# Graph attention with a residual layer norm on one core: x loads and result stores of two 128-row tiles instead of one

## The chip, the cores and the metric

The kernel runs on one core of a Trainium2 chip. The metric is the device time of one execution in microseconds (us), the median over several runs. Before the change it is 457.74 us, the median of three runs that lie between 457.65 and 457.76.

## What is computed

N = 4096 rows, D = 512 columns, all in float32. Cut to what matters:

```python
q = x @ Wq.T + bq
k = key @ Wk.T + bk
v = value @ Wv.T + bv
scores = (q @ k.T) / N ** 0.5
s = scores * adj                                   # adj is 0 or 1 and sparse
s = where(abs(s) < 1e-5, -1e9, s)
y = softmax(s, axis=-1) @ v @ Wm.T + bm
out = layernorm(x + y)
```

## The kernel before, in words

The rows of x are dealt to T = 35 tiles of R = 118 rows, padded to 128 rows in DRAM, so that each tile meets at most 256 distinct columns of the adjacency. The program has two halves.

**First half.** TensorE (PE) multiplies Wv by Wm (line 635) and then the values by the product (line 584, `value_rows`), giving a table of 4096 x 512 that ScalarE (ACT) stores to DRAM. Meanwhile GpSimd (POOL) loads the adjacency tiles (`load_adj`, line 461, 944 KB each after the cast), and VectorE (DVE) reduces each to a list of the columns in use (`reduce_tile`, line 1077 and after).

**Second half.** A loop `for i in range(T + 1)`, written out once per engine, works on one tile per step. Step i holds, on PE: the transposes of the gathered key rows and adjacency columns of tile i + 1 (lines 694, 704), the product with the values of tile i - 2 (line 737), four matmuls of a query block (`project`, line 594), the scores of tile i + 1 (line 713), and the transposes of the probabilities of tile i (line 724). POOL gathers keys six tiles ahead, values up to three. DVE does `soften(i)`, in which `key_bias(i + 1)` (line 1199) is the first reader of the x tile i + 1, and `add_x(i - 2)` (line 1288), which adds the x tile to the attention output, writes `y_buf`, and is the last reader of that x tile. From step 31 on, `add_x` is one tile nearer. ACT normalises finished tiles (`finish`, line 969), four per group of statistics.

**The queue around the change.** SyncE (SP) only issues DMAs, in the order of its own program, and blocks on each wait. It starts with the weights, then `load_x` for the first XB tiles. Then in step i it issues `store(t)` for the tiles that `finish_of(i - 1)` names, in every fourth step `load_xT` (the transposed x of four tiles for the query block, line 408), and `load_x(i + XB - 1)`. The waits are these:

```python
def load_x(t):
    if t >= XB:
        sp.wait_ge(y_sb, t - XB + 1)          # add_x of the tile that held the buffer
def store(t):
    sp.wait_ge(fin_sb, t + 1)                 # ACT has normalised tile t
# DVE, key_bias(t):   dve.wait_ge(x_in[t % XB], 16 * (t // XB + 1))
# DVE, add_x(t):      dve.wait_ge(stored[t % YB], 16 * (t // YB))   for t >= YB
```

`x_buf` has XB = 5 tiles of 2 KB per partition, `y_buf` YB = 8. The last tile is stored in two halves of its columns, one by ACT (line 965) and one by SP (line 436); after that SP waits for all stores (line 440). The code under `overflow` handles a graph that does not fit the lists; with these inputs it does not run.

Of the kernel before, what the change touches and what calls it, by code (L numbers as in the profile page):

```python
# [12 lines left out]
P = 128  # L13
N = 4096
D = 512
DC = D // P
T = 35
TP = 36
R = 118
ROWS = T * P  # L20
QR = 4 * R
# [22 lines left out]
AD = 6  # L44
XB = 5
YB = 8
# [25 lines left out]
def build(nc, adj_tiles, adj_cols, key, valueT, x, xT, wq, wk, wv, wmT, bm, consts, table, out):  # L72
    with ExitStack() as ctx:
# [3 lines left out]
        def sem(name):  # L77
            return ctx.enter_context(nc.semaphore(name))
# [106 lines left out]
        cols_in = [sem(f"cols_in{i}") for i in range(2)]  # L185
        x_in = [sem(f"x_in{i}") for i in range(XB)]
        adj_gathered = [sem(f"adj_gathered{i}") for i in range(AD)]
        key_gathered = [sem(f"key_gathered{i}") for i in range(KD)]
        v_gathered = [sem(f"v_gathered{i}") for i in range(VD)]
        stored = [sem(f"stored{i}") for i in range(YB)]  # L190

# [106 lines left out]

        x_tiles = x.rearrange("(t r) d -> t r d", r=P)
        out_tiles = out.rearrange("(t r) d -> t r d", r=P)  # L300
        table_blocks = table.rearrange("(b r k) d -> b r k d", k=4, r=P)
# [17 lines left out]

        def one_tile(ap, t):  # L320
            return ap[bass.ds(t, 1)].rearrange("a p d -> p (a d)")

        def wait_apart(eng, s, value):
            eng.wait_ge(s, value)
            eng.sem_inc(passed, 1)
# [78 lines left out]
        @block.sync  # L404
        def _(sp):
            def load_xT(nb):
                sp.wait_ge(q_ps, DC * (nb - 1))
                sp.dma_start(xT_buf[nb % 2], xT[nb]).then_inc(cols_in[nb % 2], 16)

            def load_x(t):  # L410
                if t >= XB:
                    sp.wait_ge(y_sb, t - XB + 1)
                sp.dma_start(x_buf[:, t % XB, :], x_tiles[t]).then_inc(x_in[t % XB], 16)

            def store(t):
                sp.wait_ge(fin_sb, t + 1)
                sp.dma_start(out_tiles[t], y_buf[:, t % YB, :]).then_inc(stored[t % YB], 16)

            for e in range(DC):
                sp.dma_start(v_left[:, e, :], wv[e * P:(e + 1) * P, :]).then_inc(weights2_in[e], 16)  # L420
            sp.dma_start(cst[:, :], consts).then_inc(cst_in, 16)
            sp.dma_start(bm_row[:, :], bm).then_inc(bm_in, 16)
            sp.dma_start(w_left, wq.rearrange("(e p) d -> p e d", p=P)).then_inc(weights_in, 16)
            sp.dma_start(w_right, wk.rearrange("(e p) d -> p e d", p=P)).then_inc(weights_in, 16)
            for t in range(XB):
                load_x(t)
            for i in range(T + 1):
                for t in finish_of(i - 1):
                    store(t)
                if i % 4 == 0 and i // 4 + 2 < QBL:  # L430
                    load_xT(i // 4 + 2)
                if i >= 1 and i + XB - 1 < T:
                    load_x(i + XB - 1)
            store(T - 2)
            sp.wait_ge(last_sb, 1)
            sp.dma_start(out_tiles[T - 1][:, HD:D], y_buf[:, (T - 1) % YB, HD:D]).then_inc(stored[(T - 1) % YB], 16)
            sp.wait_ge(rounds_ready, 1)
            rounds = sp.value_load(rounds_i[0:1, 0:1], min_val=0, max_val=MAXR)
            for i in range(YB):
                sp.wait_ge(stored[i], 16 * (len(range(i, T, YB)) + (i == (T - 1) % YB)))  # L440
            sp.sem_inc(again, 1)

            with overflow(sp, rounds) as n:
                with sp.Fori(0, n) as r:
                    with sp.Fori(0, QBL) as nb:
                        wait_apart(sp, g_q_sb, (r * QBL + nb) * DC + 1)
                        sp.dma_start(g_xT, xT[bass.ds(nb, 1)].rearrange("a p d n -> p (a d) n")).then_inc(g_xT_in, 16)
                sp.wait_ge(g_p_all, 2)
                with sp.Fori(0, T) as t:
                    sp.dma_start(y_buf[:, 0, :], one_tile(x_tiles, t)).then_inc(g_x_in, 16)  # L450
                    wait_apart(sp, g_fin, t + 1)
                    sp.dma_start(one_tile(out_tiles, t), y_buf[:, 1, :]).then_inc(g_stored, 16)
                    wait_apart(sp, g_stored, t * 16 + 16)

# [389 lines left out]
        def _(act):  # L844
# [114 lines left out]
            def finish_half(t):  # L959
# [4 lines left out]
                act.wait_ge(fin_sb, T)  # L964
                act.dma_start(out_tiles[t][:, 0:HD], y_buf[:, t % YB, 0:HD]).then_inc(stored[t % YB], 16)

# [70 lines left out]
        def _(dve):  # L1037
# [156 lines left out]
            def key_bias(t):  # L1194

                dve.wait_ge(x_in[t % XB], 16 * (t // XB + 1))
                if t >= 1:
# [81 lines left out]
            def add_x(t):  # L1279
# [4 lines left out]
                if t >= YB:  # L1284
                    dve.wait_ge(stored[t % YB], 16 * (t // YB))
                dve.wait_ge(r_denom_sb, t + 1)
# [199 lines left out]
def layout(rows, adj, key, value, x, Wq, Wk, Wv, Wm, bq, bk, bv, bm):  # L1486
# [25 lines left out]
    for i, b in enumerate((bq, bk, bv)):  # L1512
# [5 lines left out]
        "valueT": np.ascontiguousarray(value.reshape(NB, P, 4, DC, P).transpose(0, 4, 3, 2, 1)).reshape(NB, P, DC, 512),  # L1518
        "x": x_rows[:T].reshape(ROWS, D),
        "xT": np.ascontiguousarray(x_rows[:, :R].reshape(QBL, QR, DC, P).transpose(0, 3, 2, 1)),  # L1520
# [28 lines left out]
```

## Time and profile before

| | |
|---|---|
| median of three runs | 457.74 us |
| span of the profiled execution | 486.1 us |
| PE busy | 444.0 us, 91% of the span |
| DVE / ACT / POOL busy | 65% / 39% / 51% |
| DMA queue of SP (q1) | 12866 packets, 28.51 MB, 16.4% of the 16 engines' span |
| DMA queue of POOL (q0) | 18480 packets, 70.45 MB, 57.6% |
| x loads, result stores | 35 and 34 DMAs of 256 KB, one packet of 2 KB per partition |

The profiled execution is another execution than the timed ones and carries the recording. Its own time is given only as its span, from the first to the last instruction; that span is 28.4 us longer than the median. In the views a row has the line of the kernel, the engine, the operation, what is written and read, and its busy time. A DMA queue's share is the time of its packets over the time of 16 DMA engines. What the page calls "another core or an unknown queue" (`remote` in a wait) is a wait whose releasing event the records do not tell.

### The profile page before, as it was taken

Reading aid. Unit: us, or ns where it says so; the run is one execution under the profiler, and the core shown is the slowest. Engines: PE = TensorE matmul, PEld = TensorE weight load, DVE = VectorE, ACT = ScalarE, POOL = GpSimd, SP = SyncE. Lnnn points to the kernel's source line nnn. Section 1 sums busy time; section 2 is a strip of 40 time slices with the busy share of each in tenths; the row PEclk is TensorE's granted clock in tenths of the full one; section 3 lists DMA queues with packets and bytes.
Section 4 is the critical chain, followed back from the end, with each engine's and each line's share of the span. In section 5 each row is a group of like instructions: output and inputs, shape, how many; then the busy total and the mean of one; then the engine's idle time right before and its main releaser. Section 6 shows DMA issues by size and latency. Waiting matters only on the chain.

```text
span 486.1 us, 5650 instructions
## 1 busy us (share of the span) xinstructions
PE 444.0 (91%) x1536; PEld 246.8 (51%) x1536; DVE 317.3 (65%) x923; ACT 191.2 (39%) x447; POOL 248.6 (51%) x251
## 2 busy tenths in 40 slices
PE   9999999999999889999889798998979899889982
PEld 5444444444444455666455465655645455555651
DVE  0258535993487067989997685976937675435684
ACT  1232413433341433434443353453444345335573
POOL 2110005007672166877777776766766666661410
PEclk9999999999999998999999899999989999998997
DMA  8999999999999999998999866999757566562553
GB/s 329 363 221 285 283 290 257 226 267 316 332 311 343 268 281 241 248 285 242 229 239 321 267 188 241 257 249 324 200 150 245 166 204 227 165 212 80 156 188 112
DMA packets 34693, 119.25 MB, mean 245 GB/s; under 512 B 6767, under 2 KB 7023, under 8 KB 32610
## 3 DMA queue, kind: packets, MB, share of 16 engines
q0 software_dynamic: 18480, 70.45, 57.6%
q1 hardware_dynamic: 12866, 28.51, 16.4%
q10 hardware_dynamic: 3312, 19.89, 10.3%
q8 instruction: 14, 0.23, 0.2%
q14 instruction: 21, 0.17, 0.1%
HBM read 139.78 MB, written 17.56 MB: 324 GB/s over the span
## 4 chain that ended last, share of the span: by engine, by line
PE 63%; DVE 14%; another core or an unknown queue 8%; ACT 8%; issue 6%; ACTq 0%; DVEq 0%
PE bank L584 23%; PE bank L594 15%; PE bank L713 8%; PE bank L737 5%; PE bank L635 3%; PE bank L647 3%; PE bank L694 3%; ACT keyT L922 2%; DVE stats L1296 2%; ACT y_buf L969 2%; ACT qT L906 2%; DVE big L1077 1%; PE bank L724 1%; DVE score L1261 1%
## 5 line engine op out<-in xcount | busy, mean ns | idle before, releaser
L594 PE MATMUL bank<-big,M 128*128 128x472 f32 (+1 forms) x288 | 125.0, 562 | 8.4 <-ACT qT L906 7.4
L584 PE MATMUL bank<-y_buf,big 128*128 128x512 f32 x256 | 111.6, 594 | 0.7 <-ACT y_buf L881 0.7
L481 POOL DMA_INDIRECT v_g<-table,index x70 | 73.6, 1052 | 70.2 <-PE bank L737 20.6
L470 POOL DMA_INDIRECT key_g<-key,index x70 | 75.8, 1082 | 21.4 <-issue 21.4
L713 PE MATMUL bank<-keyT,qT 128*118 128x256 f32 x280 | 70.8, 398 | 15.1 <-ACT keyT L922 8.5
L492 POOL DMA_INDIRECT adj_g<-adj_cols,index x70 | 71.3, 1018 | 21.3 <-issue 21.3
L594 PEld LDWEIGHTS bank<-big,M 128*128 128x128 f32 x288 | 52.9, 195 | 57.1 <-issue 43.2
L584 PEld LDWEIGHTS bank<-y_buf,big 128*128 128x128 f32 x256 | 48.1, 190 | 59.4 <-issue 57.9
L713 PEld LDWEIGHTS bank<-keyT,qT 128*118 128x118 f32 x280 | 51.5, 188 | 42.1 <-ACT keyT L922 16.9
L461 POOL DMA_DIRECT2D big<-adj_tiles x35 | 19.9, 571 | 103.2 <-PE bank L584 68.1
L1077 DVE TENSOR_TENSOR big<-big 128x1888 bf16<-128x1888 bf16 x35 | 39.8, 1138 | 42.0 <-DMA big<-adj_tiles 42.0
L737 PE MATMUL bank<-v_g,probT 128*118 128x512 f32 x136 | 64.0, 593 | 0.5 <-ACT probT L948 0.5
L1259 DVE TENSOR_SCALAR size<-size 118x256 f32<-118x256 f32 x35 | 11.8, 336 | 56.7 <-ACT size L934 48.3
L922 ACT ACTIVATE keyT<-bank 128x512 f32<-128x512 f32 x70 | 37.8, 592 | 26.1 <-remote 17.5
L906 ACT ACTIVATE qT<-bank,u_col 128x472 f32<-128x472 f32 (+1 forms) x36 | 23.2, 644 | 56.1 <-PE bank L594 44.3
L694 PEld LDWEIGHTS bank<-cst,key_g 128*128 128x128 f32 x280 | 32.6, 141 | 15.1 <-issue 13.1
L694 PE MATMUL bank<-cst,key_g 128*128 128x128 f32 x280 | 36.4, 273 | 0.7 <-ACT qT L906 0.7
L948 ACT ACTIVATE probT<-bank 128x236 f32<-128x236 f32 x35 | 12.9, 368 | 58.9 <-PE bank L724 25.3
L737 PEld LDWEIGHTS bank<-v_g,probT 128*118 128x118 f32 x136 | 22.3, 182 | 17.6 <-issue 16.8
L942 ACT ACTIVATE score<-score,new_max 118x256 f32<-118x256 f32 x35 | 17.8, 508 | 34.0 <-DVE new_max L1264 25.2
L859 ACT ACTIVATE qT<-bank 128x512 f32<-128x512 f32 x20 | 12.0, 598 | 45.2 <-PE bank L584 42.8
L1254 DVE SCALAR_TENSOR_TENSOR score<-bank,c_cols,adjT 118x256 f32<-118x256 f32 x35 | 16.7, 478 | 17.7 <-PE bank L713 12.5
(124 smaller groups left out, 510.5 us busy)
## 6 DMA issues: line engine op xcount, KB each, us to landing
big<-adj_tiles POOLq DMA_DIRECT2D x35, 944.0 KB
x_buf<-x SPq DMA_DIRECT2D x35, 256.0 KB
out<-y_buf SPq DMA_DIRECT2D x34, 256.0 KB
big<-valueT ACTq DMA_DIRECT2D x8, 1024.0 KB
big<-xT SPq DMA_DIRECT2D x7, 944.0 KB
table<-qT ACTq DMA_DIRECT2D x5, 1024.0 KB
table<-y_buf ACTq DMA_DIRECT2D x3, 1024.0 KB
big<-xT ACTq DMA_DIRECT2D x2, 944.0 KB
```

The source lines that it names most:

```text
L461: pool.dma_start(adj_buf[t % AB][:, 0:AW], adj_tiles[t]).then_inc(adj_in[t % AB], 16)
L470: pool.indirect_dma_start(key_g[:, b, c, :], None, key, bass.IndirectOffsetOnAxis(index[:, t, c:c + 1], 0), bounds_check=N - 1, oob_is_err ...
L481: pool.indirect_dma_start(v_g[:, b, c, :], None, table, bass.IndirectOffsetOnAxis(index[:, t, c:c + 1], 0), bounds_check=N - 1, oob_is_err ...
L492: pool.indirect_dma_start(adj_g[:, b, c, :], None, adj_cols, bass.IndirectOffsetOnAxis(index[:, t, CH + c:CH + c + 1], 0),).then_inc(adj_g ...
L584: mm = nc.tensor.matmul(bank[4 + t % 2][:, :], col_buf[nb % 2][:, d, k * P:(k + 1) * P], G[:, d, :], start=(d == 0), stop=(d == DC - 1))
L594: mm = nc.tensor.matmul(ps[:, 0:n], M[:, d, a * P:(a + 1) * P], xT_buf[nb % 2][:, d, 0:n], start=(d == 0), stop=(d == DC - 1))
L694: nc.tensor.transpose(key_bank[c][:, a * P:(a + 1) * P], key_g[:, t % KD, c, a * P:(a + 1) * P], ident)
L713: mm = nc.tensor.matmul(bank[3][0:R, 0:SLOTS], qT[:, t // 4 % QB, a, t % 4 * R:(t % 4 + 1) * R], keyT[:, a, :], start=(a == 0), stop=(a == ...
L737: mm = nc.tensor.matmul(value_bank(t)[0:R, :], probT[:, t % 2, c * R:(c + 1) * R], v_g[:, t % VD, c, :], start=(c == 0), stop=(c == CH - 1))
L906: nc.scalar.activation(qT[:, nb % QB, a, 0:n], ps[:, 0:n], ACT.Identity, bias=u_col[:, a:a + 1]).then_inc(q_sb, 1)
L922: nc.scalar.activation(keyT[:, :, c * P:(c + 1) * P], key_bank[c][:, :].rearrange("p (a k) -> p a k", a=DC), ACT.Copy).then_inc(keyT_sb, 1)
L1077: nc.vector.tensor_tensor(t1[:, 0:H1], a[:, 0:H1], a[:, AW - H1:AW], ALU.logical_or).then_inc(adj_used, 1)
```

## The change

Two tiles share one DMA. In DRAM, x and the result are laid out as pairs: row r of tile 2b and row r of tile 2b + 1 lie next to each other, so each partition reads or writes one run of 4 KB. `x_buf` grows to XB = 6 tiles (three pairs). A pair's load is issued in even steps when `add_x` of both tiles that held its buffers is done. A pair's store is issued when its second tile is normalised. Semaphores are per pair. Tile 34, the last, is loaded together with a padding tile that nothing else reads; it is still stored alone, in two halves, on a semaphore of its own.

```diff
-ROWS = T * P
+PAIRS = TP // 2
+ROWS = TP * P
...
-XB = 5
+XB = 6
...
-        x_in = [sem(f"x_in{i}") for i in range(XB)]
+        x_in = [sem(f"x_in{i}") for i in range(XB // 2)]
...
-        stored = [sem(f"stored{i}") for i in range(YB)]
+        stored = [sem(f"stored{i}") for i in range(YB // 2)]
+        last_stored = sem("last_stored")
...
-        x_tiles = x.rearrange("(t r) d -> t r d", r=P)
-        out_tiles = out.rearrange("(t r) d -> t r d", r=P)
+        x_pairs = x.rearrange("(b r k) d -> b r k d", r=P, k=2)
+        out_pairs = out.rearrange("(b r k) d -> b r k d", r=P, k=2)
...
             def load_x(t):
                 if t >= XB:
-                    sp.wait_ge(y_sb, t - XB + 1)
-                sp.dma_start(x_buf[:, t % XB, :], x_tiles[t]).then_inc(x_in[t % XB], 16)
+                    sp.wait_ge(y_sb, t - XB + 2)
+                sp.dma_start(x_buf[:, t % XB:t % XB + 2, :], x_pairs[t // 2]).then_inc(x_in[t % XB // 2], 16)
 
             def store(t):
                 sp.wait_ge(fin_sb, t + 1)
-                sp.dma_start(out_tiles[t], y_buf[:, t % YB, :]).then_inc(stored[t % YB], 16)
+                sp.dma_start(out_pairs[t // 2], y_buf[:, t % YB - 1:t % YB + 1, :]).then_inc(stored[t % YB // 2], 16)
...
-            for t in range(XB):
+            for t in range(0, XB, 2):
                 load_x(t)
             for i in range(T + 1):
                 for t in finish_of(i - 1):
-                    store(t)
+                    if t % 2:
+                        store(t)
                 if i % 4 == 0 and i // 4 + 2 < QBL:
                     load_xT(i // 4 + 2)
-                if i >= 1 and i + XB - 1 < T:
-                    load_x(i + XB - 1)
+                if i % 2 == 0 and i >= 2 and i + XB - 2 < T:
+                    load_x(i + XB - 2)
             store(T - 2)
             sp.wait_ge(last_sb, 1)
-            sp.dma_start(out_tiles[T - 1][:, HD:D], y_buf[:, (T - 1) % YB, HD:D]).then_inc(stored[(T - 1) % YB], 16)
+            sp.dma_start(out_pairs[(T - 1) // 2][:, 0, HD:D], y_buf[:, (T - 1) % YB, HD:D]).then_inc(last_stored, 16)
...
-            for i in range(YB):
-                sp.wait_ge(stored[i], 16 * (len(range(i, T, YB)) + (i == (T - 1) % YB)))
+            for i in range(YB // 2):
+                sp.wait_ge(stored[i], 16 * len(range(i, T // 2, YB // 2)))
+            sp.wait_ge(last_stored, 32)
...
-                dve.wait_ge(x_in[t % XB], 16 * (t // XB + 1))
+                if t % 2 == 0:
+                    dve.wait_ge(x_in[t % XB // 2], 16 * (t // XB + 1))
...
-                    dve.wait_ge(stored[t % YB], 16 * (t // YB))
+                    dve.wait_ge(stored[t % YB // 2], 16 * (t // YB))
```

On SP, steps 4 to 10 of the loop stood like this before (`x_buf<-x` is `load_x`, `out<-y_buf` is `store`, `big<-xT` is `load_xT`; `y_sb` counts the `add_x` done, `fin_sb` the tiles normalised, `q_ps` the query pieces multiplied):

```order
L408 DMA big<-xT 128x1888 [waits q_ps]
L413 DMA x_buf<-x 128x512 [waits y_sb] x4
L417 DMA out<-y_buf 128x512 [waits fin_sb] x2
L408 DMA big<-xT 128x1888 [waits q_ps]
L413 DMA x_buf<-x 128x512 [waits y_sb]
L417 DMA out<-y_buf 128x512 [waits fin_sb]
```

and so they stand now:

```order
L410 DMA big<-xT 128x1888 [waits q_ps]
L415 DMA x_buf<-x 128x1024 [waits y_sb] x2
L419 DMA out<-y_buf 128x1024 [waits fin_sb]
L410 DMA big<-xT 128x1888 [waits q_ps]
L415 DMA x_buf<-x 128x1024 [waits y_sb]
L419 DMA out<-y_buf 128x1024 [waits fin_sb]
```

The four loads ahead of the first store (steps 4 to 7) have become two of double size (steps 4 and 6). So the store of tiles 0 and 1 and the xT load behind it, in step 8, stand behind the load of step 6 and no longer behind that of step 7.

At the end of SP's program, before:

```order
L413 DMA x_buf<-x 128x512 [waits y_sb]
L417 DMA out<-y_buf 128x512 [waits fin_sb] x10
L436 DMA out<-y_buf 128x256 [waits last_sb]
L438 TENSOR_LOAD rounds_i [waits rounds_ready]
L398 COMPARE_AND_BRANCH [waits stored5,stored4,stored6,stored3,stored7,stored2,stored0,stored1]
```

and now:

```order
L415 DMA x_buf<-x 128x1024 [waits y_sb]
L419 DMA out<-y_buf 128x1024 [waits fin_sb] x5
L439 DMA out<-y_buf 128x256 [waits last_sb]
L441 TENSOR_LOAD rounds_i [waits rounds_ready]
L400 COMPARE_AND_BRANCH [waits stored3,last_stored,stored2,stored0,stored1]
```

Ten stores of one tile, 24 to 33, have become five of two. Tile 32 now leaves together with tile 33, when 33 is normalised.

## Rows read from the trace of the kernel before

**Rows 1.** The page: busy time by engine, then the span in 40 slices.

```profile
span 486.1 us, 5650 instructions
PE 444.0 (91%) x1536; PEld 246.8 (51%) x1536; DVE 317.3 (65%) x923; ACT 191.2 (39%) x447; POOL 248.6 (51%) x251
DMA  8999999999999999998999866999757566562553
```

**Rows 2.** Stretches: start:end, length, busy us per engine, PEclk, DMA share, GB/s.

```profile
20.00:160.00 140.00, 138.89 (x345) 63.36 (x346) 86.75 (x195) 44.49 (x107) 41.60 (x46) 1.00 1.03 285
200.00:260.00 60.00, 55.73 (x230) 34.28 (x230) 54.78 (x164) 24.25 (x59) 47.82 (x47) 1.00 0.93 252
260.00:330.00 70.00, 63.54 (x247) 37.71 (x246) 51.91 (x165) 31.58 (x75) 49.95 (x50) 0.98 0.85 251
400.00:460.00 60.00, 53.38 (x223) 33.83 (x223) 30.72 (x111) 26.93 (x67) 30.79 (x32) 0.97 0.55 171
460.00:486.00 26.00, 15.02 (x67) 9.31 (x65) 17.12 (x59) 15.32 (x35) 3.94 (x4) 0.91 0.46 155
```

**Rows 3.** The chain that ended last, shares of the span by engine.

```profile
PE 63%; DVE 14%; another core or an unknown queue 8%; ACT 8%; issue 6%; ACTq 0%; DVEq 0%
```

**Rows 4.** The tile x_buf: its readers, and what ended idle time before them.

```profile
L1199 DVE CUSTOM_DVE_ANT_0 big<-x_buf,w_row,kappa x35: 731/743/774, 158.4 to 466.6; 118x512 f32<-118x512 f32 x35
...
  PE bank L737: 2.2, 1
  issue: 0.3, 1
```

**Rows 5.** Waits: DVE's longest for a DMA; SP's own for buffers and results.

```profile
DVE big L1077 <- DMA big<-adj_tiles: 42.0, 12, 11.0
SPq L413 <- DVE y_buf L1288: 197.5, 21, 31.0
SPq L417 <- ACT y_buf L969: 18.9, 8, 5.1
```

**Rows 6.** Timeline, 443 to 461 us: loads of tiles 32, 33; their first reads.

```profile
443.34 0.34 SPq L413 DMA_DIRECT2D x_buf<-x  x1
451.44 0.34 SPq L413 DMA_DIRECT2D x_buf<-x  x1
452.43 0.74 DVE L1199 CUSTOM_DVE_ANT_0 big<-x_buf,w_row,kappa 118x512 f32<-118x512 f32 x1
460.27 0.74 DVE L1199 CUSTOM_DVE_ANT_0 big<-x_buf,w_row,kappa 118x512 f32<-118x512 f32 x1
```

**Rows 7.** DMA, 443 to 448 us, in 40 slices of 0.125 us; packets, MB, share.

```profile
DMA  0000000000039054469999999861000000000000
q1 hardware_dynamic: 288, 0.52, 31.1%
```

**Rows 8.** DMA packets, MB and share, 16 to 20 us: 2 KB packets alone.

```profile
q1 hardware_dynamic: 844, 1.62, 105.4%
```

**Rows 9.** The same, 9 to 14 us: 8 KB packets of q10 beside q1.

```profile
q10 hardware_dynamic: 213, 1.61, 77.1%
q1 hardware_dynamic: 217, 0.45, 23.2%
```

**Rows 10.** The same, 31 to 35 us: packets of the adjacency tiles alone.

```profile
q0 software_dynamic: 125, 0.88, 105.0%
```

**Rows 11.** The end: SP's stores of tiles 31 to 33, of the last half.

```profile
478.78 3.33 SPq L417 DMA_DIRECT2D out<-y_buf  x3
482.16 0.43 SPq L436 DMA_DIRECT2D out<-y_buf  x1
```

**Rows 12.** DMA, 478.5 to 486.2 us, in 40 slices of 0.19 us.

```profile
DMA  0000019997999100000006999999911300000000
q1 hardware_dynamic: 576, 0.92, 32.8%
q10 hardware_dynamic: 144, 0.13, 5.1%
```

More of the change, by code:

```diff
@@ L318, in build, with one_half @@
         V_USES = [V_SLOT.count(i) for i in range(VS)]
-        def one_tile(ap, t):
-            return ap[bass.ds(t, 1)].rearrange("a p d -> p (a d)")
+        def one_half(ap, pair, k):
+            return ap[bass.ds(pair, 1), :, k, :].rearrange("a p d -> p (a d)")
         def wait_apart(eng, s, value):
@@ L448, in _ @@
                 sp.wait_ge(g_p_all, 2)
[L449 to L453, printed above, removed]
+                with sp.Fori(0, T // 2) as pair:
+                    for k in range(2):
+                        sp.dma_start(y_buf[:, 0, :], one_half(x_pairs, pair, k)).then_inc(g_x_in, 16)
+                        wait_apart(sp, g_fin, pair * 2 + (k + 1))
+                        sp.dma_start(one_half(out_pairs, pair, k), y_buf[:, 1, :]).then_inc(g_stored, 16)
+                        wait_apart(sp, g_stored, pair * 32 + (k + 1) * 16)
+                sp.dma_start(y_buf[:, 0, :], x_pairs[T // 2][:, 0, :]).then_inc(g_x_in, 16)
+                sp.wait_ge(g_fin, T)
+                sp.dma_start(out_pairs[T // 2][:, 0, :], y_buf[:, 1, :]).then_inc(g_stored, 16)
+                sp.wait_ge(g_stored, T * 16)
         @block.gpsimd
@@ L964, in finish_half @@
                 act.wait_ge(fin_sb, T)
-                act.dma_start(out_tiles[t][:, 0:HD], y_buf[:, t % YB, 0:HD]).then_inc(stored[t % YB], 16)
+                act.dma_start(out_pairs[t // 2][:, 0, 0:HD], y_buf[:, t % YB, 0:HD]).then_inc(last_stored, 16)
             def finish(t):
@@ L1518, in layout @@
         "valueT": np.ascontiguousarray(value.reshape(NB, P, 4, DC, P).transpose(0, 4, 3, 2, 1)).reshape(NB, P, DC, 512),
-        "x": x_rows[:T].reshape(ROWS, D),
+        "x": np.ascontiguousarray(x_rows.reshape(PAIRS, 2, P, D).transpose(0, 2, 1, 3)).reshape(ROWS, D),
         "xT": np.ascontiguousarray(x_rows[:, :R].reshape(QBL, QR, DC, P).transpose(0, 3, 2, 1)),
@@ L1543 @@
     r = run_bass_kernel_spmd(nc, [arrays], core_ids=[0])
-    tiles = r.results[0]["out"].reshape(T, P, D)
+    tiles = r.results[0]["out"].reshape(PAIRS, P, 2, D).transpose(0, 2, 1, 3).reshape(TP, P, D)
     result = np.empty((N, D), np.float32)
```

## The prediction, made before the changed kernel was run

> **What bounds the kernel now.** I read the busy times first, then the stretches, the chain, and last the waits around x.
>
> The page shows PE busy for 91% of the span, and the DMA engines at eight or nine tenths up to the middle, then falling to five or six [rows 1]. Both could be the bound, so the stretches decide. From 20 to 160 us PE is busy for 138.89 of 140 us although the DMA share is 1.03 [rows 2]: PE sets that time and a faster DMA has at most 1.1 us to give. From 200 to 330 us PE is at 55.73 of 60 and 63.54 of 70; DVE is at 54.78 of 60 in the first of these, because it still reduces adjacency tiles beside the softmax. From 400 us on, DMA is at 0.55 and PE at 53.38 of 60. What PE lacks in these three stretches is 4.3, 6.5 and 6.6 us, and the question is whether an x load or a store is behind any of it.
>
> The chain gives 63% to PE, 14% to DVE, 8% to ACT, and 8% (39 us) to waits whose releasing event is not recorded [rows 3]. No DMA of x or of the result is named. The tile x_buf says it directly: `key_bias`, the first reader of each x tile, and `add_x` are preceded by idle time of DVE for PE (2.2 us, once) and for an instruction's issue (0.3 us), and never for a load [rows 4]. DVE does wait 42.0 us for DMAs, but for adjacency tiles. SP waits 197.5 us for buffers of x to be given back and 18.9 us for finished tiles [rows 5]: SP is always early, and nobody waits for it.
>
> The span is 28.4 us above the median. I make the sum against the span, and carry the difference over to the median. The unrecorded waits, 39 us, are enough to be this surplus; nothing here proves it.
>
> **The change, part by part.**
>
> *Packets.* Of 16 to 20 us, 1.62 MB in 2 KB packets took 105.4% of 16 engines [rows 8]: 67.5 us over 791 packets, 85 ns each. In 9 to 14 us 1.61 MB in 8 KB packets took 77.1% [rows 9]: 61.7 us over 197, 313 ns each. No row has a 4 KB packet of SP's queue. Two of 85 ns give 170 ns, half of 313 gives 157; I take 162, nearer to the middle, so a pair saves 8 ns (0 to 13). 17 loads and 17 stores of pairs merge 34 x 128 = 4352 pairs of packets: 4352 x 8 / 16 = 2.2 us of all engines' time (0 to 3.5). The padding tile costs 128 x 77 / 16 = 0.6 us. That is 1.6 us less DMA work (0.6 more to 2.9 less), spread over the whole run. It lies beside PE, and I cost it at nothing; if the engines were the bound it would be 1.6.
>
> *Start.* Three pairs instead of five tiles are 0.25 MB more, 8 x 77 ns = 0.6 us on each engine, ahead of the first adjacency tiles. They hit DVE, which then has 42.0 us of waiting in hand [rows 5]; PE runs on the values and is not touched. Zero.
>
> *Issue.* SP issues 34 DMAs fewer at 0.34 us each [rows 6]. SP is idle for most of the run. Zero. In the loop the first stores and the xT loads go out up to a step earlier, which adds slack.
>
> *Even tiles.* The load of tiles t and t + 1 waits for `add_x(t - 5)`, just what tile t alone waited for; tile t + 1 comes a step earlier than before. So only the even tile is at risk, by the longer transfer. The load of tile 32 is issued at 443.34 and first read at 452.43, 9.1 us later; for tile 33 it is 8.8 us [rows 6]. How long would 512 KB take? Beside the load of tile 32 a store of the same size was issued: the two moved 0.52 MB from 444.4 to 446.6 us, so the last packet went out 3.3 us after the first issue [rows 7]. With about 1 us more to the event, some 4.8 us of the 9.1 are left. Zero.
>
> *Beside adjacency tiles* the queues take turns. In 9 to 14 us q10 moved 213 packets and q1 217, though q10's were 8 KB [rows 9]: one packet each in turn. An adjacency packet takes 67.2 us / 117 = 577 ns [rows 10]. A tile has 8 packets per engine, and a pair also 8, only longer. So 8 x (577 + 85) = 5.3 us becomes 8 x (577 + 162) = 5.9 us, with start and event some 8 us, still under 8.8. The pair takes hardly longer than the tile alone.
>
> The Trainium skill, "DMA: Bandwidth & Descriptors", section "Queues, rings and completion order", says that an engine turns between queues at packet boundaries, and that a packet typically holds 9 to 17 descriptors. The first half agrees with [rows 9]. By the second an x transfer would hold an engine through a whole DMA at a turn, 8 x 162 ns = 1.3 us against 0.7, and a gather behind it would come 0.6 us later; the near equal counts in [rows 9] speak against it.
>
> *End.* This is the one place where nothing hides a transfer. Before, tiles 31 and 32 left ahead of tile 33: two bursts are seen, the first from 479.5 us, the second from 482.5 to 484.1 [rows 12]. SP issued the store of 33 as the last of three that end at 482.11, and the last half at 482.16 [rows 11]. Now tile 32 waits for 33 and joins the second burst. That is 128 packets of 4 KB for 128 of 2 KB, 8 x (162 - 85) = 0.6 us more on each engine, and the last half is behind it in the same queue. If the end is set by something else than the queue this is 0; if the packets are worth two of 85, 0.7. I take 0.6. After it SP passes 5 instead of 8 semaphores, at most 0.1 us less.
>
> Sum: 486.1 + 0.6 - 0.1 = 486.6 us for the span, **457.74 + 0.5 = 458.2 us** for the median.
>
> **The rivals.**
>
> *A. The DMA work or the unrecorded waits count (faster).* For it: DMA shares of 0.85 to 1.03 up to 330 us [rows 2], and 39 us of waits that no row explains [rows 3]. If they come from crowded queues, half as many DMAs on SP would shorten them. Against: PE at 99% in the stretch with the highest share, and no DMA of x named. Price: 1.6 us of engine time, to 2.9, and a tenth of 39 us is 3.9. Taking 2.9: about 455.3 us. Chance 0.2.
>
> The Trainium skill, again "DMA: Bandwidth & Descriptors", section "Anatomy of one DMA — SWDGE (gpsimd) path", gives a DMA a fixed 2 us beside its bytes. By that 34 DMAs fewer would be 68 us less if they ran one after another. Here they lie beside PE: [rows 7] show two at once, and [rows 4] nobody waiting. I give a gain from it no more than 0.02, inside A.
>
> *B. A pair lands too late (slower).* `key_bias` stands in DVE's order ahead of the softmax, so a late pair stops DVE, then ACT and PE. The place is steps 8, 12 and 16, where `load_xT` is just ahead in the same queue and adjacency tiles are still coming. Its packets, priced as 8 KB, add 8 x (577 + 313) = 7.1 us: 15.1 us to the landing. The point that decides is a lead of 8.8 to 9.1 us. Beyond it each of three pairs costs up to 6 us; at half of that, 9 us in all: 467 us. Against: the xT load now leaves up to a step ahead of the pair, not just before it. Chance 0.07.
>
> *C. Gathers come later (slower).* In its turn an x packet holds an engine 162 instead of 85 ns, 0.3 us for a gather of some four packets per engine. If values were just in time, 17 pairs x 0.3 = 5 us: 463 us. Against: there are half as many turns, and the gathers go out tiles ahead. Chance 0.05.
>
> *D. The packets stay at 2 KB.* Then the last store is 16 x 85 instead of 8 x 162 ns long, 0.7 us: 458.4 us, not to be told from the forecast by time. Chance 0.05, within my case.
>
> **The numbers.** A measurement of this kernel can tell about 0.2%, 0.9 us, from no change. My case, with D, has 0.68: 457.5 to 458.9 us, of which 0.08 goes beyond 458.65, into slower. So faster 0.2, same 0.6, slower 0.08 + 0.07 + 0.05 = 0.2. The range takes in most of A and the near part of C: 455.3 to 460.5 us.
>
> **What would show it.** Right: idle time before L1199 without a DMA; 4 KB packets near 162 ns in SP's queue; PE at 138.9 of 140 in the same stretch; the last burst some 0.6 us longer, and the store of the pair 32, 33 issued some 0.7 us before the last half. Wrong: a wait of DVE for x_buf, above all at even tiles after 250 us (B); less PE idle time from 200 to 460 us, or fewer unrecorded waits with a median lower by more than 0.9 us (A); PE waiting before L737 for v_g (C).

## The result, and the profile after

The changed kernel takes 458.56 us, the median of 20 runs (457.77 to 460.37). The kernel before, in as many runs beside it, takes 457.69 us (457.01 to 459.37). The ratio is 1.0022, with a 95% interval of 1.0012 to 1.0031: the change makes the kernel 1.0 us slower (0.5 to 1.4), by the ratio. The forecast was 458.2, 0.5 us slower. It has the side right and the size about half, and the measured 0.22% lies on the border of what I had called no change. Two further sets of runs (e2 and e11 below) give ratios of 1.0003 and 0.9998, because there the kernel before had long executions that it has not in these 20; so the size holds for this set, and what follows rests on the traces.

The page of the changed kernel, busy times and the DMA slices [rows 1]:

```profile
span 457.9 us, 5598 instructions
PE 434.0 (95%) x1536; PEld 245.5 (54%) x1536; DVE 317.9 (69%) x923; ACT 190.5 (42%) x447; POOL 246.9 (54%) x251
DMA  8999999999999999999899988699978577666443
```

Its stretches, with the columns of [rows 2]:

```profile
20.00:160.00 140.00, 138.97 (x345) 62.91 (x344) 86.18 (x194) 45.09 (x108) 42.29 (x47) 1.00 1.03 285
200.00:260.00 60.00, 55.85 (x231) 34.44 (x230) 54.71 (x164) 25.07 (x60) 47.20 (x47) 1.00 0.96 272
260.00:330.00 70.00, 70.00 (x286) 43.59 (x285) 61.86 (x190) 35.11 (x85) 54.77 (x54) 1.00 0.91 281
400.00:440.00 40.00, 39.10 (x177) 25.69 (x177) 27.03 (x95) 23.35 (x56) 23.17 (x23) 1.00 0.63 201
```

Its chain [rows 3]:

```profile
PE 82%; DVE 10%; ACT 3%; issue 2%; DMA 1%; DVEq 0%; ACTq 0%
```

This execution took 459.67 us, 1.8 more than its span. So a span can be set beside a time, and the span of 486.1 us ahead of the prediction belonged to a disturbed execution: the waits without a recorded release, 8% there, are gone here. That is not the change's doing. The kernel before, traced again, shows the same:

```profile
span 455.9 us, 5650 instructions
PE 433.2 (95%) x1536; PEld 245.1 (54%) x1536; DVE 316.8 (69%) x923; ACT 190.4 (42%) x447; POOL 246.5 (54%) x251
```

```profile
20.00:160.00 140.00, 139.21 (x346) 63.47 (x347) 86.81 (x195) 45.06 (x108) 41.03 (x46) 1.00 1.03 285
200.00:260.00 60.00, 55.77 (x230) 34.36 (x229) 54.77 (x164) 25.77 (x62) 47.61 (x47) 1.00 0.93 258
260.00:330.00 70.00, 70.00 (x293) 44.12 (x292) 60.52 (x189) 34.50 (x83) 54.64 (x54) 1.00 0.93 292
```

This is the third trace of the kernel before (run e7 below; its execution took 457.69 us). What the reader is to see: in both kernels PE is busy for all of 260 to 330 us and for 139 of 140 us from 20 to 160, and from 200 to 260 us it lacks the same 4.2 us. The middle is PE's, with or without the change, and the difference must lie at the start or at the end. Of the 2.0 us between these two spans, 1.5 lie ahead of the first key transposes of the second half (at 168.2 us here, at 166.8 in the kernel before) and 0.7 behind the last value product; e2 returns to the start.

The reads of x in the changed kernel [rows 4] still have no load before them, and SP still waits for others [rows 5], now longer for tiles to be normalised (64.9 us; 20.7 in e7). With only the loads paired (e4) it is 57.7, with only the stores 22.4 (e5), so it comes from the loads: SP is no longer held up by those of odd steps. The rows of x_buf, and then SP's waits:

```profile
L1209 DVE CUSTOM_DVE_ANT_0 big<-x_buf,w_row,kappa x35: 733/742/783, 159.8 to 438.0; 118x512 f32<-118x512 f32 x35
...
  PE bank L746: 2.2, 1
  DVE r_denom L1287: 0.3, 1
...
DMA to landing us min/median/max: 3.2/5.6/16.5
```

```profile
SPq L415 <- DVE y_buf L1298: 209.1, 15, 38.2
SPq L419 <- ACT y_buf L978: 64.9, 17, 6.1
```

The end of the changed kernel: the last value product, the pair stores, the last tile's halves on SP and on ACT [rows 11].

```profile
447.16 1.96 PE L752 MATMUL bank<-v_g,probT 128*118 128x256 f32 x8 [0.32 <-ACT probT L957]
450.20 2.81 SPq L419 DMA_DIRECT2D out<-y_buf  x2
453.19 1.04 SPq L439 DMA_DIRECT2D out<-y_buf  x1
453.38 0.35 ACTq L974 DMA_DIRECT2D out<-y_buf  x1
```

and its DMA from 450.3 to 458 us, in slices of 0.19 us, with the time from ACT's issue to landing [rows 12]:

```profile
DMA  0003999999303000498999989996131000000001
q1 hardware_dynamic: 432, 1.18, 40.0%
out<-y_buf ACTq DMA_DIRECT2D x1, 128.0 KB, 3.6
```

The same end in the kernel before, third trace, DMA from 449.7 to 455.7 us, in slices of 0.15 us:

```profile
445.91 1.96 PE L743 MATMUL bank<-v_g,probT 128*118 128x256 f32 x8 [0.32 <-ACT probT L948]
448.94 2.81 SPq L417 DMA_DIRECT2D out<-y_buf  x3
451.94 1.16 SPq L436 DMA_DIRECT2D out<-y_buf  x1
452.13 0.35 ACTq L965 DMA_DIRECT2D out<-y_buf  x1
```

```profile
DMA  3999899998100300089996996199611200000000
q1 hardware_dynamic: 576, 0.92, 42.4%
out<-y_buf ACTq DMA_DIRECT2D x1, 128.0 KB, 3.1
```

Measured from the end of the last value product (449.12 and 447.87 us), ACT issues its half 4.26 us later in both. The two halves share a semaphore, so the 3.6 and 3.1 us run to the landing of both, the last tile as a whole: 7.86 us in the changed kernel (453.38 + 3.6 - 449.12), 7.36 in the kernel before (452.13 + 3.1 - 447.87). The last packets are those of SP's half, which stands behind the pair in SP's queue: from 455.9 us on the profile has 15 packets of q1 and none of ACT's q10. The span ends at 8.8 and at 8.0. So 0.5 us of the 0.7 to 0.8 is the landing, and about 0.3 lies behind it.

The first trace of the kernel before, the disturbed one, is nearer to the changed kernel here: the last tile lands at 7.7 us and the span ends at 8.4. Over all traces with single stores (before, e1, e4, e7, e9, e10) the landing lies at 6.9 to 7.7 us and the end at 7.9 to 8.4; over those with paired stores in runs of 4 KB (the changed kernel three times, e5, e6; e8, which holds back more, apart) at 7.8 to 8.0 and 8.5 to 9.0. The two groups do not overlap.

### The profile page after: what moved, and what is told of

The parts are those of the page before. It is cut to its first block, busy times and chain, and to the rows that moved or that the text cites. A ratio compares the mean times of both kernels' runs of the same rounds, so it can differ in the third digit from the quotient of the medians.

```text
span 457.9 us, 5598 instructions
## 1 busy us (share of the span) xinstructions
PE 434.0 (95%) x1536; PEld 245.5 (54%) x1536; DVE 317.9 (69%) x923; ACT 190.5 (42%) x447; POOL 246.9 (54%) x251
## 4 chain that ended last, share of the span: by engine, by line
PE 82%; DVE 10%; ACT 3%; issue 2%; DMA 1%; DVEq 0%; ACTq 0%
PE bank L593 24%; PE bank L603 21%; PE bank L722 11%; PE bank L746 10%; PE bank L703 6%; PE bank L644 4%; PE bank L656 3%; PE bank L733 2%; PE bank L713 1%; DVE big L1086 1%; DVE stats L1306 1%; DMA qT<-wmT 1%; ACT keyT L931 1%; DVE score L1271 1%; DVE big L1088 1%
## 5 line engine op out<-in xcount | busy, mean ns | idle before, releaser
L603 PE MATMUL bank<-big,M 128*128 128x472 f32 (+1 forms) x288 | 121.7, 550 | 0.3 <-ACT y_buf L868 0.3
L479 POOL DMA_INDIRECT key_g<-key,index x70 | 74.1, 1059 | 21.6 <-issue 21.3
L501 POOL DMA_INDIRECT adj_g<-adj_cols,index x70 | 70.5, 1007 | 21.3 <-issue 20.7
L470 POOL DMA_DIRECT2D big<-adj_tiles x35 | 19.9, 570 | 104.4 <-PE bank L593 67.9
L722 PE MATMUL bank<-keyT,qT 128*118 128x256 f32 x280 | 66.6, 381 | 6.7 <-DVE score L1264 4.9
L722 PEld LDWEIGHTS bank<-keyT,qT 128*118 128x118 f32 x280 | 50.5, 182 | 29.4 <-issue 16.8
L703 PEld LDWEIGHTS bank<-cst,key_g 128*128 128x128 f32 x280 | 32.6, 141 | 15.1 <-issue 13.1
L1298 DVE SCALAR_TENSOR_TENSOR y_buf<-bank,r_denom,x_buf 118x512 f32<-118x512 f32 x34 | 25.5, 751 | 2.5 <-PE bank L746 2.2
```

Of the source, the lines that this page charges most:

```text
L479: pool.indirect_dma_start(key_g[:, b, c, :], None, key, bass.IndirectOffsetOnAxis(index[:, t, c:c + 1], 0), bounds_check=N - 1, oob_is_err ...
L501: pool.indirect_dma_start(adj_g[:, b, c, :], None, adj_cols, bass.IndirectOffsetOnAxis(index[:, t, CH + c:CH + c + 1], 0),).then_inc(adj_g ...
L603: mm = nc.tensor.matmul(ps[:, 0:n], M[:, d, a * P:(a + 1) * P], xT_buf[nb % 2][:, d, 0:n], start=(d == 0), stop=(d == DC - 1))
L703: nc.tensor.transpose(key_bank[c][:, a * P:(a + 1) * P], key_g[:, t % KD, c, a * P:(a + 1) * P], ident)
L722: mm = nc.tensor.matmul(bank[3][0:R, 0:SLOTS], qT[:, t // 4 % QB, a, t % 4 * R:(t % 4 + 1) * R], keyT[:, a, :], start=(a == 0), stop=(a == ...
L1298: nc.vector.scalar_tensor_tensor(y, value_bank(t)[0:R, :], r_denom[0:R, t:t + 1], x_buf[0:R, t % XB, :], ALU.mult, ALU.add).then_inc(y_sb, 1)
```

## The experiments

The sections below give the median of 12 runs (13 for e9) and the ratio to the kernel before, which is not the quotient of two medians. The kernel before was run 35 times beside each of three sets, with medians of 457.98 us (e1 to e4), 459.09 (e5 to e8, on another chip) and 459.00 (e9 to e12). Such a ratio has an interval of about 0.002 to 0.003 each way here, wider than the effect. The verdicts therefore rest on the traces, in particular on two stretches: from the first key transposes of the second half to the last value product ("the middle"), and from there to the end of the span ("the end"). "The half lands" means below that both halves of the last tile have landed, counted from the last value product.

The first theories are T (the cost is at the end, in the last pair's store), S (at the start, in the larger loads) and M (in the middle). T2 is T after the first four runs, with a second term behind the landing.

**e1, the kernel before.** No edit.

> The kernel before, unchanged, for a second trace and as a measure of the noise: its ratio to the kernel before should be 1.000 within 0.001. Theory T (the end: the last pair's store) expects a span some 0.5 to 0.6 us under that of the changed kernel's trace (457.9), with the whole difference behind TensorE's last value product; the span should lie near 457 and not near 486. Theory S (the start) expects the first product of the values by G (which began at 20.15 us in the trace of before and at 21.93 us in that of the changed kernel) to begin at 20.1 to 20.3 here, 1.7 us ahead of the changed kernel, as in the first trace. Theory M (the middle) expects less idle time of TensorE between 160 and 440 us than the 10 us of the changed kernel.

Measured: 459.05 us, ratio 1.0010 (0.9982 to 1.0037). The first value product begins at 19.9 us and the end is 8.3 us long, but this execution took 460.42 us (span 458.6, not the 457 that T expected), and its middle 284.0. The trace has a wait that the first one had not shown:

```profile
270.56 0.75 DVE L1199 CUSTOM_DVE_ANT_0 big<-x_buf,w_row,kappa 118x512 f32<-118x512 f32 x1 [2.90 <-DMA x_buf<-x]
```

DVE waits 2.90 us for the load of tile 12, and PE then idles 1.7 us. Against the 281.1 us of e7 the middle is 2.9 us longer; 0.9 of it had arisen by 188 us, behind a spell of 3.4 us from 183.8 in which PE's clock was granted at half (1.2 instead of 2.4 GHz). The stretch 184 to 188 us in e1, and in e7:

```profile
184.00:188.00 4.00, 3.59 (x9) 1.79 (x8) 3.20 (x8) 1.24 (x4) 3.19 (x3) 0.60 1.03 259
184.00:188.00 4.00, 3.02 (x14) 1.70 (x13) 3.19 (x9) 1.30 (x5) 3.09 (x4) 1.00 1.04 271
```

PE had been idle for 2.27 us up to 182.6 us in e1, and for 2.28 us up to 183.0 in e7, where the clock stayed up.

The late load is my rival B, a load that lands too late behind an xT load and stores, but in the kernel *before*. The SP queue of this run, and under it that of the changed kernel:

```profile
238.01 10.54 SPq L413 DMA_DIRECT2D x_buf<-x  x2
248.59 0.94 SPq L417 DMA_DIRECT2D out<-y_buf  x2
249.58 0.53 SPq L408 DMA_DIRECT2D big<-xT  x1
255.33 0.34 SPq L413 DMA_DIRECT2D x_buf<-x  x1
```

```profile
238.93 0.33 SPq L415 DMA_DIRECT2D x_buf<-x  x1
242.24 0.34 SPq L419 DMA_DIRECT2D out<-y_buf  x1
242.63 0.48 SPq L410 DMA_DIRECT2D big<-xT  x1
255.89 0.33 SPq L415 DMA_DIRECT2D x_buf<-x  x1
```

Two single stores and the xT load go out at 248.6 to 250.1 us and are still moving when tile 12 is asked for at 255.3. In the changed kernel they go out at 242.2, because the load of step 7 no longer stands ahead of them (in e4, with only the loads paired, at 239.5; in e5, with only the stores, at 248.1). Its load of tiles 12 and 13, twice as large, lands 10.2 us after its issue and is first read 2.5 us later.

**e2, the changed kernel.** No edit.

> The changed kernel, unchanged. Ratio 1.001 to 1.003 to the kernel before. T: from the end of TensorE's last value product to the end of the wait for the stores some 7.9 us or more, 0.5 longer than in the kernel before. S: the first product of the values by G again at 21.9 us, and TensorE's full clock again granted only at 9.5 us; if it begins at 20.2 here, the late start was that one execution's and not the change's.

Measured: 459.20 us, ratio 1.0003 (0.9976 to 1.0029), less than the 1.001 expected. The end is 8.75 us, as in the first trace, and the half lands at 7.8. The value products begin at 22.2 us here, at 19.4 in e11, and at 19.3 to 20.7 in e3, e6, e8 and e12, all with the same start; in the kernel before at 19.9 to 20.5. PE's full clock (2.4 GHz, granted clock 1.0 instead of 0.5) is granted at 9.5 and 9.9 us where they begin near 22, and at 4.6 in e11. So the start differs between executions of one kernel by up to 2.8 us, and the change does not by itself make it late: theory S falls as the cause of the change's cost. Whether late starts are more frequent with it, these traces cannot tell.

**e3, tiles 32 and 33 stored singly.**

```diff
-            store(T - 2)
+            sp.wait_ge(fin_sb, T - 2)
+            sp.dma_start(out_pairs[(T - 3) // 2][:, 0, :], y_buf[:, (T - 3) % YB, :]).then_inc(last_stored, 16)
+            sp.wait_ge(fin_sb, T - 1)
+            sp.dma_start(out_pairs[(T - 3) // 2][:, 1, :], y_buf[:, (T - 2) % YB, :]).then_inc(last_stored, 16)
```

(SP's last waits are counted to match.)

> The changed kernel with tiles 32 and 33 stored one by one (runs of 2 KB into the pair layout), as in the kernel before; all else as changed. T: 0.5 to 0.6 us under the changed kernel, ratio 1.0005 to 1.001 to the kernel before. S and M: as the changed kernel, ratio 1.002, since the start and the middle are untouched.

Measured: 458.43 us, ratio 1.0002 (0.9983 to 1.0022). The end is 8.5 us, and the last half lands at 7.6 after the last value product. That is 0.25 us off the changed kernel's end, half of what T expected. The 0.3 us behind the landing stay. The store of tiles 30 and 31 still goes out as a pair, tile 30 later than before, which may be the rest; no run shows it.

**e4, only the loads paired.**

```diff
-XB = 5
+XB = 6
...
-                    sp.wait_ge(y_sb, t - XB + 1)
-                sp.dma_start(x_buf[:, t % XB, :], x_tiles[t]).then_inc(x_in[t % XB], 16)
+                    sp.wait_ge(y_sb, t - XB + 2)
+                sp.dma_start(x_buf[:, t % XB:t % XB + 2, :], x_pairs[t // 2]).then_inc(x_in[t % XB // 2], 16)
...
-                if i >= 1 and i + XB - 1 < T:
-                    load_x(i + XB - 1)
+                if i % 2 == 0 and i >= 2 and i + XB - 2 < T:
+                    load_x(i + XB - 2)
```

> The kernel before with only the x loads paired (six x buffers, 4 KB runs); the stores stay single. T: no difference from the kernel before, ratio 1.000 within 0.001. S, if the larger x loads at the start are its cause: the full 1.002. M, if the loads are its cause (even tiles later, gathers behind longer packets): 1.001 to 1.002, with a wait of VectorE ahead of the first reader of x or of TensorE for gathers.

Measured: 458.02 us, ratio 0.9989 (0.9970 to 1.0009). No wait for x; the middle is 281.0 us, the end 7.9, no longer than in the kernel before. So the longer end comes with the stores.

**e5, only the stores paired.** The mirror image of e4: XB stays 5, the loads stay single. The diff, cut, is against the kernel before.

```diff
-                sp.dma_start(out_tiles[t], y_buf[:, t % YB, :]).then_inc(stored[t % YB], 16)
+                sp.dma_start(out_pairs[t // 2], y_buf[:, t % YB - 1:t % YB + 1, :]).then_inc(stored[t % YB // 2], 16)
...
-                    store(t)
+                    if t % 2:
+                        store(t)
```

> The changed kernel with the x loads as in the kernel before (five buffers, one tile each, 2 KB runs) and only the stores paired. The revised theory T2 has two terms behind TensorE's last value product: the last half lands some 0.6 to 0.8 us later (7.8 us after that product instead of 6.9 to 7.2), and SP goes from its last branch to its end in 0.49 instead of 0.18 us. Both come with the stores and the code of SP, so T2 expects 8.7 to 8.8 us from the last value product to the end of the span, and a ratio of 1.001 to 1.003. Rival L (the loads are what costs) expects 7.9 to 8.4 us there and a ratio of 1.000. If the wait of VectorE for x at tile 12 belongs to single loads, it can show here again.

Measured: 458.50 us, ratio 0.9971 (0.9944 to 0.9998). The end is 9.0 us and the last half lands at 8.0: T2 holds there, rival L does not. The part of T2 on SP's last branch does not hold: it takes 0.18 us here, and 0.45 us pass between SP's last two waits instead. The wait for tile 12 is back, 0.4 us, so it belongs to the single loads. The ratio below 1 goes with the slow median of the kernel before in this set, 459.09 us.

**e6, the changed kernel without SP's code for the case that does not occur.**

```diff
-            with overflow(sp, rounds) as n:
-                with sp.Fori(0, n) as r:
...
-                sp.wait_ge(g_stored, T * 16)
```

> The changed kernel without the code on SP that handles a graph that does not fit the lists; with these inputs it never runs. T2: the step from SP's last wait to its end shrinks from 0.6 us (branch to end 0.49) to 0.3 or less, the landing of the last half stays at 7.8 us behind the last value product, and the span behind that product comes to some 8.4; ratio to the kernel before 1.0010 to 1.0017 instead of 1.002. If the step does not shrink, the 0.3 us are not the code's place or length.

Measured: 458.25 us, ratio 0.9959 (0.9938 to 0.9980), beside the same runs of the kernel before as e5. The half lands at 7.8 us as before, and the end is 8.5 us instead of 8.75. SP itself comes to the end of its program 0.5 us sooner after the landing, but all engines meet there before the span ends, and now DVE is the last to come:

```profile
L74 SPq DRAIN  x1: 7/7/7, 456.3 to 456.3; - x1
L74 DVEq DRAIN  x1: 59/59/59, 456.5 to 456.5; - x1
```

In the changed kernel it is SP (457.6 us, DVE 457.4). So 0.2 us of the end go with code of SP that never runs, and DVE bounds the gain.

**e7, the kernel before, a third time.**

> The kernel before, once more: ratio 1.000 within 0.003. It is to tell whether VectorE's wait of 2.9 us for the load of tile 12, seen in the trace of the second run of the kernel before, is there in every execution. Theory W (it is an accident of some executions) expects it shorter or absent here, with the time from the first key transposes to the last value product at 281 to 282 us as in the four kernels with paired loads or stores; rival V (it is always there, and the change gains it) expects it again, 2 to 3 us, and 282.5 or more.

Measured: 459.97 us, ratio 1.0002 (0.9969 to 1.0035), over runs from 457.51 to 463.71. Its trace is the one shown above. The middle is 281.1 us, the same as with the change (280.9 to 281.1), and the wait for tile 12 is 0.44 us:

```profile
267.50 0.75 DVE L1199 CUSTOM_DVE_ANT_0 big<-x_buf,w_row,kappa 118x512 f32<-118x512 f32 x1 [0.44 <-DMA x_buf<-x]
```

Theory W holds and V falls. The load of tile 12 lands just as it is asked for; e7 loses nothing by it on PE, e1 1.7 us.

**e8, four tiles held back to the end.**

```diff
-                    if t % 2:
+                    if t % 2 and t != T - 4:
                         store(t)
...
+            sp.wait_ge(fin_sb, T - 1)
+            store(T - 4)
             store(T - 2)
```

> The changed kernel with the store of tiles 30 and 31 held back until tile 33 is normalised, so that two pairs leave together ahead of the last half: the suspected cost made larger by 8 packets of 4 KB on each DMA engine. T2: 8 x 165 ns = 1.3 us more behind the last value product than the changed kernel (10.0 to 10.1 us instead of 8.75), ratio 1.004 to 1.006. If the end is set by a fixed latency and not by the queue, no change: 8.75 us and 1.002.

Measured: 459.90 us, ratio 1.0012 (0.9985 to 1.0039). From the last value product (ends at 447.63) to the end of the span (457.7) it is 10.1 us, 1.3 more than in the changed kernel:

```profile
445.67 1.96 PE L754 MATMUL bank<-v_g,probT 128*118 128x256 f32 x8 [0.31 <-ACT probT L959]
451.17 0.81 SPq L419 DMA_DIRECT2D out<-y_buf  x2
452.03 0.78 SPq L441 DMA_DIRECT2D out<-y_buf  x1
```

This is the price of the term, made large: 8 packets of 4 KB on every engine, held back, are 8 x 165 ns, and the landing too is 1.3 us later. The end is set by the queue and not by a fixed latency. The ratio is below the 1.004 expected, which goes with the slow median of the kernel before in this set; of the runs beside it, its fastest quarter lies at 459.55 us, against 458.40 for e5 and 458.11 for e6 on the same chip.

**e9, six single buffers.**

```diff
-XB = 5
+XB = 6
```

> The kernel before with six x buffers instead of five, all else single. Each load goes out one step earlier, so that tile 12 is no longer read as it lands. Theory Q (the kernel before loses time in disturbed executions because the load of tile 12 stands behind two stores and the xT load, and the change mends this) expects no wait of VectorE for x, the slow executions above 460 us gone, and the fastest ones as before, 457.0 to 457.5, since the end is untouched (8.0 to 8.3 us behind the last value product). Rival N (the slow executions of the kernel before are noise of the chip) expects the same spread as the kernel before, up to 462 or 463.

Measured: 458.68 us, ratio 0.9988 (0.9967 to 1.0008). The wait for x is gone. But one of its 13 runs took 463.41 us, and the trace fell on it. Nothing of x is late there. From the first value product to the first key transposes of the second half it takes 5.9 us longer than e7. PE waits there for the column lists that DVE makes from the adjacency tiles, and near the end of that wait, at 89.6 us, its clock falls to half (1.2 GHz) for 6.8 us:

```profile
81.31 1.14 DVE L1077 TENSOR_TENSOR big<-big 128x1888 bf16<-128x1888 bf16 x1 [3.80 <-DMA big<-adj_tiles]
89.93 0.59 PE L614 MATMUL bank<-cell_count,cst 128*128 128x1 f32 x2 [2.42 <-DVE big L1106]
```

So theory Q, by which the late load is the cause of the long executions, is not enough, though of the other 12 runs none is above 459.53 us. The fastest is 457.77, not in the 457.0 to 457.5 expected.

**e10, the paired loads again.** As e4.

> The kernel before with only the loads paired, once more, beside the changed kernel on one chip. T2 and Q expect it to have both gains: fastest executions 0.7 to 1.0 us under the changed kernel's (457.0 to 457.3), no wait for x, no executions above 460, and a ratio to the kernel before of 0.996 to 0.999; 7.9 to 8.1 us behind the last value product.

Measured: 458.04 us, ratio 0.9985 (0.9966 to 1.0003), all runs between 457.23 and 459.43. The end is 8.0 us.

**e11, the changed kernel, a third time.**

> The changed kernel, once more: 8.7 to 8.8 us behind the last value product, the last half landing at 7.8; fastest executions 0.7 to 1.1 us above the fastest of the kernel before, and none above 461. N expects its spread to be that of the kernel before.

Measured: 458.70 us, ratio 0.9998 (0.9975 to 1.0022), 458.06 to 460.13. The middle is 281.1 us and the end 8.7, the third time within 0.1 us. The ratio is 1 again, and in this set the median of the kernel before is 0.3 us the higher one.

**e12, pairs in runs of 2 KB.**

```diff
-        x_pairs = x.rearrange("(b r k) d -> b r k d", r=P, k=2)
-        out_pairs = out.rearrange("(b r k) d -> b r k d", r=P, k=2)
+        x_pairs = x.rearrange("(b k r) d -> b r k d", r=P, k=2)
+        out_pairs = out.rearrange("(b k r) d -> b r k d", r=P, k=2)
```

> The changed kernel's DMAs, waits and buffers, but the tile layout of the kernel before in memory, so that each pair moves in runs of 2 KB: the run length alone is undone. T2: the last half lands as in the changed kernel or up to 0.1 us later (16 x 87 against 8 x 165 ns), 7.8 to 7.9 us behind the last value product, and the time is the changed kernel's within 0.2 us; the packets of SP's queue are 85 to 88 ns each, so that 4 KB save 5 to 10 ns per pair. Rival R (the run length is what matters) expects it to differ from the changed kernel by 0.5 us or more, either way.

Measured: 459.00 us, ratio 1.0006 (0.9983 to 1.0030). The end is 8.9 us with 512 packets of 2 KB at 87 ns in the place of 256 of 4 KB at 165; the half lands at 7.5, 0.3 us earlier than T2 expected, and only in this one trace; why is open. The end is long all the same because DVE comes to the last meeting of the engines at 456.5 us, 0.5 after SP. Against e11 in the same set the median is 0.3 us higher. That lies within the spread: no gain from undoing the run length is seen, and rival R's 0.5 us is not either.

**A version to keep.** In all, the kernel before ran 149 times, the changed kernel 44 times, and the version with only the loads paired 24 times. The medians are 458.69, 458.60 and 458.03 us; the fastest quarters end at 457.69, 458.47 and 457.70. Above 460.4 us, the slowest run of the changed kernel, lie 26 of the 149 and none of the others; 12 of the 26 are in the set on the other chip, where neither of the two ran (e5 and e6 did: none of 24). So these pooled medians must not be set against each other. Within a set the changed kernel's median is 0.9 us above that of the kernel before in the first, 1.2 above in the second (459.20 against 457.98) and 0.3 below in the third (458.70 against 459.00). Pairing the loads alone has the fastest quarter of the kernel before and the narrow spread of the change. Its median lies below that of the changed kernel beside it, by 1.2 us in the second set and 0.7 in the third. Its two intervals (0.9970 to 1.0009 and 0.9966 to 1.0003) still contain 1, so it is not shown to beat the kernel before.

## Why the prediction was right or wrong

*What bounds the kernel.* Right, and more strictly than I had it: PE is busy for 70.00 of 70 us from 260 to 330 in either kernel. The idle time of PE that I counted at 6.5 us there was that of a disturbed execution. I had noted that its span was 28.4 us above the median, and that the unrecorded waits could be this surplus. In every later trace of this kernel both are gone together, which makes it likely and does not show it.

*Packets.* I took 162 ns for 4 KB. From 451.0 to 452.4 us of the changed kernel there are only such packets and 13 tiny ones:

```profile
q1 hardware_dynamic: 139, 0.52, 92.7%
```

20.8 us over 126 packets is 165 ns, against 2 x 85 [rows 8]. A pair of 2 KB packets joined saves 5 ns and not 8. The term of zero on the path stands, since the middle is 281.1 us in e7 and in e11. (Two slips in the sums change nothing: 67.2 us over 117 packets is 574 ns, not 577, and rival D, with the 0.1 us for semaphores taken off as in my own case, comes to 458.3 us.)

*Start, issue.* Right: zero, as far as a start that varies by 2.8 us by itself lets one see.

*Even tiles.* Right in its result: the load of tiles 32 and 33 is issued at 415.02 and lands at 419.5, well ahead of the first read at 423.85, 4.4 us in hand where I had 4.8. No row had given the "about 1 us more to the event" in that sum; at the end of the runs the last packet and the landing lie 0.4 to 0.7 us apart.

```profile
415.02 0.33 SPq L415 DMA_DIRECT2D x_buf<-x  x1
423.85 0.74 DVE L1209 CUSTOM_DVE_ANT_0 big<-x_buf,w_row,kappa 118x512 f32<-118x512 f32 x1
```

But the sentence under it, that nobody waits for SP, was wrong of the kernel before. "The point that decides is a lead of 8.8 to 9.1 us" took the lead from the end of the run, where the queue is empty. At tile 12 the lead is longer and the queue fuller: in e1 its load took 15.2 us, near the 15.1 that I had priced in rival B for a load of twice the size, which is luck, and it was already late. The change mends this, and I had put it down as a mere "adds slack". None of my rows could show it: in the first trace DVE reads tile 12 15.1 us after the load's issue and does not wait.

*End.* This is the term that decides. Its mechanism is as I had it: the pair makes SP's queue longer ahead of the last half, and nothing hides it. Its first part, 0.6 us for the transfer, was about right in size: the half lands 0.5 us later than in e7, 0.6 than in e4, 1.0 than in e1 (and only 0.1 than in the first, disturbed trace), and e8 gives 1.3 us for a whole pair held back, 0.65 for the part that tile 32 adds. Its second part was mis-sized. I had taken off 0.1 us for fewer semaphores, but from the landing to the last branch SP takes 0.18 us in the changed kernel and 0.16 in e7. In its place the runs show some 0.3 us more from the landing to the end of the span (0.9 against 0.6 to 0.7 in e7, e4 and e10), of which e6 takes off 0.2. It is not a clean term: e5 had 1.0 us there with a branch of 0.18, and in e1 (1.4), e9 (1.3) and e12 (1.5) DVE, not SP, was the last at the meeting of the engines.

In sum the end is 8.75 us against 8.0 in e7 and 8.3 in e1, 0.5 to 0.7 us more, and 0.8 more than in e4 and e10, whose loads are the same (7.9 and 8.0). The fastest quarters of the pooled runs lie 0.8 us apart, from the kernel before and from e4 with e10 alike. So against e4 and e10 the end accounts for all of it; against the kernel before 0.1 to 0.4 us of the 0.8 to 0.9 are not accounted for.

*The rivals.* A fell: no unrecorded waits, yet nothing gained. B has its mechanism right and its place wrong, as said. C did not show: PE never waits for a gather. D fell: the packets are of 4 KB, though e12 shows that the time would hardly differ.

*What stays open* is what makes the long executions of the kernel before. The late load accounts for 1.7 us of idle PE in one of them. A fall of the clock goes with them: the traces of e1, of e9 and of the first, disturbed execution each have a spell of 3.4 us at half clock that begins between 183 and 189 us, and no other trace has one there. Over the recorded runs of the kernel before, the mean granted clock is 0.990 in the 26 above 460.4 us and 0.994 in the 42 up to 458, which by my estimate (0.0036 x 461 / 0.5) is 3.3 us more at half clock. What makes it fall is not shown. The late load is not the whole cause, because e5 keeps it and has no run above 459.24, and e9 has none and has one at 463.41. That the changed kernel and its parts have so few may come from the order in SP's queue early in the run, or from something else; no run tells these apart.

## What to carry to other kernels

Where an engine is busy throughout, as PE is here, joining DMAs in the steady part was worth nothing; look at the last few, where nothing hides them, and let each result leave as soon as it is ready, since the tile that waited for its partner cost about its own transfer in front of the last store. Read the slack of a load at the place where its queue is fullest, not at the quietest: here two stores and an xT load ahead made a 256 KB load take 15 us, and a pair of twice the size, sent behind an emptier queue, took 10. And if the span of a trace is far above the timed runs, take its waits as those of another execution until a second trace shows them.

## What the runs showed of the hardware that I had not expected

- The clock of PE at the start. The full clock came at 4.0 to 9.9 us in different executions, and the first value product between 19.0 and 22.2 us with it. In the two latest (9.5 and 9.9 us) PE had been idle for 0.5 and 0.6 us between its first warm-up products and the first real one, waiting for a weight; in e4 it idled 0.7 us there, but the full clock had come before, at 4.0 us.
- The span ends when the last engine has come to a common point, and that is not always the one with the last wait: SP in the changed kernel, DVE in e1, e6, e9 and e12.
- SP's way from its last branch to its last instruction takes 0.49 us in the changed kernel in all three traces and in e3, e8 and e12, 0.18 to 0.19 in the kernel before, e4, e5 and e10, though all of these have code there that they jump over. With that code gone (e6) the branch is gone too. What in the code makes the difference is not shown.
- Issuing the last half took SP 0.33 to 1.17 us in different executions, 1.04 to 1.17 in the three traces of the changed kernel. The landing does not follow it: in e5 the issue took 0.33 us and the half landed at 8.0, in the changed kernel 1.04 and 7.8.
